# Expert loops whose bodies hold eight tiles instead of four

## What is computed

```python
xn = layernorm(x) * ln_gamma + ln_beta
abel_out = gelu(xn @ abel_w + abel_b)
topw, topi = top_k(xn @ moe_gate_w + moe_gate_b, 2)       # 2 of 8 experts for each token
w = softmax(topw)
h = gelu(xn @ ew1[e] + eb1[e])                            # e of the 8: 256 -> 512
eo = h @ ew2[e] + eb2[e]                                  # 512 -> 256
moe_out = (sum over the two experts of w * eo) @ expm(gens[0]) @ expm(gens[1]) @ expm(gens[2])
gate = sigmoid(concat(abel_out, moe_out) @ gc_w + gc_b)
out = x + abel_out * (1 - gate) + moe_out * gate
```

## Time and profile before

| | us |
|---|---|
| median of the runs | 1411.75 |
| lowest and highest | 1410.81, 1412.97 |
| the profiled execution | 1412.15 |
| its span | 1410.5 |

### The profile page before, as it was taken

The page is one execution under the profiler, slowest core; times in us unless marked ns, Lnnn a source line. Parts: engine busy times, 40 slices in busy tenths (PEclk is TensorE's granted clock), DMA queues, the critical chain, the costliest instruction groups (busy, mean ns, idle before and its releaser), DMA issues. The chain is left out here.

```text
span 1410.5 us, 25901 instructions
## 1 busy us (share of the span) xinstructions
PE 1137.2 (81%) x7112; PEld 988.3 (70%) x7113; DVE 876.6 (62%) x2780; ACT 497.6 (35%) x953; POOL 413.0 (29%) x478
## 2 busy tenths in 40 slices
PE   6796896982699999953799989997970999999930
PEld 5663674872589888952689878896860888888920
DVE  6536764887366666636776667545774566666648
ACT  1011562342244444421333333332431434444435
POOL 3001110477344444420000000001676334444410
PEclk9898997697799999986899999998885999999975
DMA  9400242258543333333011101000466753433347
GB/s 287 150 0 0 98 162 100 77 207 267 179 151 90 105 90 90 89 101 137 0 46 46 46 5 42 1 0 1 167 232 208 240 189 106 134 105 102 105 173 239
DMA packets 75432, 161.11 MB, mean 114 GB/s; under 512 B 11270, under 2 KB 36562, under 8 KB 75354
## 3 DMA queue, kind: packets, MB, share of 16 engines
q1 hardware_dynamic: 54794, 104.93, 21.8%
q0 software_dynamic: 19776, 54.45, 12.9%
q10 hardware_dynamic: 784, 0.79, 0.2%
HBM read 88.66 MB, written 71.47 MB: 114 GB/s over the span
## 5 line engine op out<-in xcount | busy, mean ns | idle before, releaser
L1451 PE MATMUL bank<-ew,rows 128*128 x852 | 300.1, 352 | 4.8 <-DVE rows L1086 3.1
L1452 PE MATMUL bank<-low_in,rows 128*128 x852 | 273.1, 321 | 0.0
L1453 PE MATMUL bank<-ew,rows 128*128 x852 | 272.8, 320 | 0.0
L1238 POOL DMA_INDIRECT results<-xh x142 | 141.6, 997 | 298.2 <-DVE xh L1114 284.3
L1451 PEld LDWEIGHTS bank<-ew,rows 128*128 128x128 f32 x852 | 161.8, 190 | 18.5 <-issue 11.6
L1453 PEld LDWEIGHTS bank<-ew,rows 128*128 128x128 f32 x852 | 161.3, 189 | 11.8
L1452 PEld LDWEIGHTS bank<-low_in,rows 128*128 128x128 f32 x852 | 162.3, 191 | 6.1
L1333 ACT ACTIVATE xh<-bank 128x512 f32<-128x512 f32 x142 | 85.0, 599 | 224.9 <-PE bank L1453 224.9
L606 POOL TENSOR_TENSOR work<-work,mhalf 128x8 f32<-128x8 f32 (+1 forms) x20 | 37.9, 1894 | 404.7 <-DVE work L599 404.7
L1123 DVE TENSOR_TENSOR rows<-bank,rows 128x512 fp32r<-128x512 f32 x142 | 98.2, 692 | 91.9 <-ACT rows L170 74.3
L1219 POOL DMA_INDIRECT slots_in<-xh,work x128 | 127.4, 995 | 49.4 <-issue 36.5
(11 more groups left out here) (317 smaller groups left out, 2031.3 us busy)
## 6 DMA issues: line engine op xcount, KB each, us to landing
xh<-slots_in POOLq DMA_DIRECT2D x142, 129.0 KB, 2.6
low_in<-low SPq DMA_DIRECT2D x32, 512.0 KB
xh<-results SPq DMA_DIRECT2D x14, 1032.0 KB, 5.3
residual<-xs SPq DMA_DIRECT2D x16, 512.0 KB, 6.3
dense<-ab SPq DMA_DIRECT2D x16, 512.0 KB, 6.5
xs<-residual SPq DMA_DIRECT2D x16, 512.0 KB, 4.7
ab<-dense SPq DMA_DIRECT2D x9, 512.0 KB, 6.3
xs<-in_L_attn_a_x_dram SPq DMA_DIRECT2D x4, 1024.0 KB
```

The lines of the kernel that those rows point to most:

```text
L1238: pool.indirect_dma_start(out=yg, out_offset=bass.IndirectOffsetOnAxis(ap=back[j % RING], axis=0), in_=yr[j % RING], in_offset=None).then_ ...
L1451: pe.matmul(o, hi, f32r(high(c)), start=(c == 0), stop=False)
L1452: pe.matmul(o, hi, f32r(low(c)), start=False, stop=False)
L1453: last = pe.matmul(o, lo, f32r(high(c)), start=False, stop=(stop and c == chunks[-1]))
```

## The change

The body of the loop takes PASS = ROUNDS x RING = 8 tiles. `TURNS` becomes 63 // 8 = 7 and `TAIL` 7 + 56 = 63, so that 8 tiles are in the unrolled tail. The first 7 tiles stay as they are. In the body k runs from 7 to 14, the tile number is `i * PASS + k` and the round `i * ROUNDS + k // RING`. Nothing else is changed: the same work is done for each tile in the same order, on the same buffers.

```diff
             FIRST = 2 * RING - 1
-            TURNS = (SLOTS - 1 - FIRST) // RING
+            ROUNDS = 2
+            PASS = ROUNDS * RING
+            TURNS = (SLOTS - 1 - FIRST) // PASS
...
-            TAIL = FIRST + TURNS * RING
+            TAIL = FIRST + TURNS * PASS
...
                 with eng.Fori(0, TURNS) as i:
-                    run([(i * RING + k, k % RING, i + k // RING) for k in range(FIRST, FIRST + RING)])
+                    run([(i * PASS + k, k % RING, i * ROUNDS + k // RING) for k in range(FIRST, FIRST + PASS)])
```

## The result

The kernel with eight tiles in a body took 1404.93 us (median of 5 runs, 1404.1 to 1405.56); the one before took 1412.33 in the 5 runs beside it (1410.81 to 1412.97). The direction was right and the size was not, so the question is where the other 3 us came from.

A forecast was written before the change was run, and what follows sets the result against it. It took TensorE to bound the two expert loops; 2.15 us from loop 1 and 2.07 from loop 2, all else counted as 0, gave 4.2 us off the 1411.75 median: 1407.5 us, 8-in-10 range 1406.0 to 1410.8.

The forecast's parts named there:

- The price of an edge: At each taken back edge TensorE pauses: 0.27 us in loop 1, 0.295 us in loop 2.
- Part 1: Eight edges go per loop: 2.15 us in loop 1, 2.07 in loop 2 with one absorbed by a wait; together 4.2.
- Parts 2 and 3: ACT's and DVE's removed edges are hidden, and the tail of 8 unrolled tiles instead of 4 changes nothing: 0 us.
- Part 4: Mid-body, at the fifth tile, the new ring round's semaphore values are worked out again: 0 us taken, at most 0.7 lost.
- rival A: The excess comes with each ring round, not the jump, and stays mid-body: half the gain, 2.1 us, 1409.7; chance 0.17.
- Part 5: Fifteen tile bodies of code become 23, more code is fetched once per loop, and straight fetching is free.
- Part 6: What follows each loop waits for its last tile, so the loops' gain reaches the end in full.
- Rival B: Longer body outgrows instruction memory; each back edge waits 2.6 us for code: 27 us slower, 1439; chance 0.10 for slower.
- C: The loop compiles unchanged, or other work at the edge replaces what is removed: 1411.7 us; chance 0.04.
- D: Larger gain because later loads in loop 2 settle better too: 6 us or more, 1405.5 us; chance 0.03.

The follow-up runs named there:

- rounds3: Kernel before with bodies of 12 tiles instead of four, so 4 taken back edges a loop instead of 14; ratio 0.9961 of the kernel before.
- long_tail: Kernel before with two turns fewer a loop (12 taken edges instead of 14) and 12 unrolled tail tiles instead of 4; ratio 0.9981.
- rounds15: Kernel before with one turn of 60 tiles, all 71 tiles written out and no back edge taken; ratio 0.9926.
- again_before: The kernel before run once more, unchanged, on another chip; ratio 0.9999.
- nudge_before: Kernel before with 12 idle instructions (fulfilled waits) added on TensorE ahead of loop 1; ratio 0.9998.
- again_after: The changed kernel (eight tiles in a body) run once more, unchanged, on another chip; ratio 0.9967 of the kernel before.
- again_after2: The changed kernel (eight tiles in a body) run a third time, unchanged; ratio 0.9955 of the kernel before.
- rounds5: Kernel before with bodies of 20 tiles instead of four, so two taken back edges a loop; ratio 1.0057.
- rounds7: Kernel before with bodies of 28 tiles instead of four, so one taken back edge a loop; ratio 1.0020.
- pad_after: Changed kernel with 224 fulfilled waits added on TensorE ahead of loop 1 and 204 ahead of loop 2; ratio 1.0121 of the kernel before.
- pad_before: Kernel before with 110 idle instructions (fulfilled waits) added on TensorE ahead of loop 1, no edge removed; ratio 0.9991.
- loop1_only: Kernel before with bodies of eight tiles in loop 1 only, loop 2 keeping bodies of four; ratio 0.9964.

## Why the prediction was wrong in size, point by point

- **The price of an edge: right.** Mean steady part of loop 1 in the four traces with before's loops 191.33, in the four with after's 189.44: 1.89 / 7 = 0.27. Loop 2: 191.43 - 189.73 = 1.70, 0.24 each, where 0.295 was taken; there rounds3, long_tail and rounds15 give 0.18 (8 edges), 0.29 and 0.29. TensorE's taken branch is 208 ns, and taking it away gives 0.24 to 0.30 us (0.18 in one case), as the pipe behind it empties.
- **Part 1, the sum of the loops: right.** Whole loops, means of four traces each: 249.65 to 247.02, 2.6; 251.82 to 250.13, 1.7: together 4.3 against the 4.2 forecast. That the two agree so well is partly luck: loop 1 gave 0.5 more than its 2.15 and loop 2 gave 0.4 less than its 2.07. The eighth edge of loop 2 lay ahead of a wait, and is absorbed on the mean: the first 16 tiles of loop 2 take 60.4 us before and 60.4 after. But the wait is not a fixture, as I had it: it sits at tile 14 before and at tiles 7, 9 and 13 after, and those 16 tiles vary from 58.5 to 62.8 us over the runs. With such a spread the means of four agree with an absorbed edge and don't show it; in one execution the luck of these loads is worth more than the edge.
- **Parts 2 and 3, hidden edges and the tail: right.** The tail's tiles keep 3.46 to 3.49 in loop 1, and nothing in the loops' gain asks for a share of ACT's and DVE's edges.
- **Part 4 and rival A: A is refuted.** The middle of a body, where the ring starts again, has no excess: 3.49 in the rows above, 3.46 to 3.50 over the loop. The value of 0 was right in the middle of a body, the bound of 0.7 was never needed. What the part didn't have is that each edge that stays costs some 0.03 to 0.05 us more (above); why is open.
- **Part 5, code: half wrong, and this is a step that failed.** "Straight fetching is free" holds inside the loops (rounds15: no tile of steady part 1 over 3.49 us). I then dropped the fetches from the account. A packet of code travels beside the data, and at both exits of the kernel before it ran on past the start of the reload, by 0.6 and 0.2 us.
- **Part 6, the exits: the step that failed.** I took what follows the last tile to be the same in both kernels and read only that it waits. It was the earlier trace rows, the 5.60 us of the scatter's landing, that I passed over: I put its change at nothing without a reason, and it became 4.31 for the same scatter. Exits 1.1 and 1.3 us shorter (7.03 to 5.92 and 11.12 to 9.82, means of before, again_before and nudge_before against after, again_after and again_after2) are 2.4 us, the missed term of the sum.
- **The sum with that term.** 4.3 + 2.4 = 6.7 us. On the other chips the change gave 4.8 (0.9967 of 1439.91) and 6.5 us (0.9955 of 1446.69), on the first 7.4. The first chip's interval, 5.1 to 9.2 us, holds 6.7, and the remaining 0.7 lies in stretches where the work is the same. The interval of the 4.8, 3.0 to 6.3 us, doesn't hold 6.7: its loops and exits gave as much as elsewhere, and what took some 2 us back outside them wasn't found. rounds15 supports the account from further out: by its stretches 4.9 + 3.7 in the loops and 0.9 + 1.3 in the exits give 10.8 us, 0.9925; measured was 0.9926, with an interval of some 2.8 us to either side.
- **Rival B: false at eight tiles, true at 20.** Neither the 564 records that the body has in the trace nor the 845 of rounds3 nor 1406 stalls TensorE; 1967 does. By these runs its limit lies between 1406 and 1967, and VectorE's between 222 (rounds3) and 368. My price of a miss, 2.6 us from a load's landing, was low: VectorE's pauses are 2.8 to 3.0 in rounds5, TensorE's 4.1 to 4.5 in rounds7, and the lower clock behind them comes on top.
- **C** is refuted by the branches' count. **D**, the larger gain, for which "nothing in the waits speaks", had the size right and the place wrong: later loads of loop 2 bring nothing on the mean. What spoke for more stood at the exits, in the packets' records.

What stays open: why the nudge of 12 instructions left the packet in its place; how an overlap of 0.2 to 0.6 us of one packet makes the reload and the scatter end 1.0 to 1.8 us later; and why pad_after's second exit lies between. That the place of the code sets the length of the exits is shown by moving it in three ways (pad_before, long_tail, loop1_only), the first without any other change. That it does so by the packet's overlap with the reload's start is inferred from the packets' records: all six long exits have the overlap and no short one has it, but no run made a short exit long. The one that tried, pad_after, brought the packet back but not past the reload's start.

## What to carry to other kernels

Price a back edge from tile distances, and put it against what the loop waits for; then cut the program also at the barriers behind the loops and ask of each landing there what else is in flight on its DMA engines, code included. A longer body pays until one of the engines has to fetch its code again at the edge, and the first to do so need not be the one that bounds the loop (here VectorE at 368 records, with TensorE at 1406 and not yet stalled): count the records of each engine between two branches. Where the whole loop can be written out, as here with 71 tiles, that was best of all: 0.9926 of the kernel before, against 0.9955 to 0.9967 for eight tiles on these chips.

## What the runs showed of the hardware

- A packet of 16 KB of TensorE's code takes 0.9 to 1.8 us over all these traces. Where it still ran as the 512 KB reload began, the reload's last packets ended 3.45 to 3.73 us after the scatter's start instead of 1.74 to 1.95, and the barrier came 1.1 us later (exit 1).
- 110 idle instructions on TensorE ahead of loop 1 (355 to 376 us) moved its code packet at exit 2, 1000 us on, from -1.25 to -7.26 us and shortened that exit from 11.23 to 9.75; 12 of them left the packets at -1.22 and -1.03.
- A loop body of 368 records on VectorE pays 2.8 to 3.0 us at each back edge, one of 222 no such pause; on TensorE a body of 1406 has a branch of 0.21 to 0.24 us, one of 1967 a branch of 4.1 to 4.5 us.
- A stall of 4.1 us of TensorE in rounds7 was followed by a granted clock of 0.71 over the next tile, which added 1.3 us to it at full work.
